# Graph attention edge pass: attention scores of four chunks in fourteen on VectorE instead of TensorE

## The reference, cut to what matters

```
x1  = layernorm(x)                      # per node, over 768
ft  = x1 (per head) @ W.T               # 12 heads, 64 -> 64
a1  = sum(ft * attn_l, -1)              # source score, one number a head
a2  = sum(ft * attn_r, -1)              # target score, one number a head
e   = leaky_relu(a1[src] + a2[dst], 0.2)
w   = exp(e - segment_max(e, dst)[dst])
msg = w / segment_sum(w, dst)[dst] * ft[src]
x   = x + relu(segment_sum(msg, dst) + x1 @ W_res.T)
x   = x + ffn(layernorm(x))
```

## Time and profile before

| | before |
|---|---|
| median of 3 runs | 2722.25 us (2721.98 to 2723.72) |
| the profiled execution | 2722.58 us, of which its span is 2720.8 us |
| busy, share of the span: PE, PEld, DVE, ACT, POOL | 97%, 88%, 88%, 87%, 78% |
| granted TensorE clock, mean | 0.989 of full |

### The profile page before, as it was taken

The page is one execution under the profiler, slowest core; times in us unless marked ns, Lnnn a source line. Parts: engine busy times, 40 slices in busy tenths (PEclk is TensorE's granted clock), DMA queues, the critical chain, the costliest instruction groups (busy, mean ns, idle before and its releaser), DMA issues. The chain is left out here.

```text
span 2720.8 us, 69258 instructions
## 1 busy us (share of the span) xinstructions
PE 2628.0 (97%) x21450; PEld 2389.0 (88%) x21450; DVE 2397.0 (88%) x4890; ACT 2378.5 (87%) x4748; POOL 2135.0 (78%) x2029
## 2 busy tenths in 40 slices
PE   5999999999999985999999999999999999999998
PEld 4888888888888864899999999999999999999997
DVE  4688888888888876999999999999999999999996
ACT  4988888888888863999999999999999999999993
POOL 7777777777777615888888888888888888888882
PEclk9999999999999997999999999999999999999999
DMA  8677777787777646899999999999999999989883
GB/s 314 215 259 254 254 252 253 252 252 253 254 253 255 217 149 245 313 350 341 333 332 330 324 321 324 324 317 315 317 321 314 314 319 315 311 312 312 315 311 119
DMA packets 254177, 777.86 MB, mean 286 GB/s; under 512 B 77185, under 2 KB 85165, under 8 KB 253837
## 3 DMA queue, kind: packets, MB, share of 16 engines
q1 hardware_dynamic: 184190, 563.88, 58.4%
q0 software_dynamic: 69312, 210.37, 25.0%
q10 hardware_dynamic: 432, 0.62, 0.1%
HBM read 638.86 MB, written 236.65 MB: 322 GB/s over the span
## 5 line engine op out<-in xcount | busy, mean ns | idle before, releaser
L1017 PE MATMUL ps<-wr_bd,arena 128*128 128x128 f32 x4704 | 592.7, 276 | 19.1 <-DVE arena L1390 19.0
L1017 PEld LDWEIGHTS ps<-wr_bd,arena 128*128 128x128 f32 x4704 | 563.0, 193 | 20.5 <-issue 20.4
L702 POOL DMA_INDIRECT arena<-agg_scratch,nrow x392 | 438.9, 1120 | 76.7 <-issue 67.5
L644 POOL TENSOR_SCALAR arena<-csr_neg,mv,r_n 128x768 f32<-128x768 f32 x392 | 388.2, 990 | 50.9 <-PE ps L859 37.9
L1385 DVE SCALAR_TENSOR_TENSOR ps<-ps,r_n,arena 128x768 f32<-128x768 f32 x392 | 398.9, 1018 | 16.6 <-DMA arena<-agg_scratch,nrow 15.5
L809 ACT ACTIVATE t_hi<-ps 128x768 fp32r<-128x768 f32 x392 | 314.3, 802 | 95.4 <-PE ps L859 95.2
L818 ACT ACTIVATE arena<-arena,s_st 128x768 f32<-128x768 f32 x392 | 363.6, 928 | 30.5 <-DVE arena L1390 30.5
L1390 DVE SCALAR_TENSOR_TENSOR arena<-ps,arena 128x768 f32<-128x768 f32 x392 | 375.3, 957 | 13.4
L692 POOL TENSOR_SCALAR arena<-arena,nm_n,r_n 128x768 f32<-128x768 f32 x392 | 382.6, 976 | 2.7 <-issue 1.9
L1397 DVE TENSOR_TENSOR t_lo<-ps,t_hi 128x768 fp32r<-128x768 f32 x392 | 373.7, 953 | 10.2 <-ACT t_hi L809 10.2
L777 ACT ACTIVATE arena<-arena,mv 128x768 f32<-128x768 f32 x392 | 367.4, 937 | 12.8
(11 more groups left out here) (213 smaller groups left out, 6218.9 us busy)
## 6 DMA issues: line engine op xcount, KB each, us to landing
arena<-in_x SPq DMA_DIRECT2D x196, 768.0 KB
arena<-in_x_cols SPq DMA_DIRECT2D x392, 384.0 KB, 5.0
out<-arena SPq DMA_DIRECT2D x195, 768.0 KB, 5.7
agg_scratch<-agg_ring SPq DMA_DIRECT2D x196, 384.0 KB, 3.8
dst_all<-in_dst_rows SPq DMA_DIRECT2D x28, 256.0 KB, 3.7
arena<-agg_scratch,nrow POOLq DMA_INDIRECT x392
arena<-in_x,e_slot POOLq DMA_INDIRECT x364, 4.6
dst_all<-in_dst_rows SPq DMA_DIRECT2D x28, 192.0 KB
```

The source lines that it names most:

```text
L644: pool.tensor_scalar(g_ring[:, g, :].rearrange("p (c f) -> p c f", f=P), csr_neg[:, None, :].to_broadcast([P, NC, P]), mv1[:, w, 2 * (v % ...
L702: pool.indirect_dma_start(g_ring[:, g, :], None, agg_d, bass.IndirectOffsetOnAxis(nrow[:, v, 3:4], 0), bounds_check=EP - 1, oob_is_err=Fal ...
L1017: last = nc.tensor.matmul(res_ps(b, tr)[:, i * P:(i + 1) * P], xt_ring[:, g, i * P:(i + 1) * P], wr_bd[:], start=True, stop=True)
```

## The change

Of every fourteen chunks, those at positions 2, 5, 9 and 12 (OFF_PE; "off chunks" from here) get their target scores without TensorE:

- ScalarE copies the target row from SBUF to `both_t`, scaled by -1/768, and sums it while it copies, which gives the negative mean.
- VectorE, as the last or one of the last operations of that step, computes (row + negative mean) * `v2_row`, where `v2_row` holds the 12 vectors of 64 side by side, the same in all partitions ("the product"); in the next step it sums the 64 numbers of each head ("the reduction").
- TensorE leaves out the six transposes of the target row, and one step later the six score matmuls and the matmul L933; the copies of their results go too, on ScalarE L745 and one of three pieces of L735 (and half of another), on VectorE L1184.
- For all chunks `ve_d` now comes behind the aggregated row, not ahead of the copy of the scores.
- `v2_row` is made once, at the pass's start: a product and a copy of 768 columns on VectorE, two matmuls on TensorE.

By i mod 7 the transposes go at steps 0 and 4, the score matmuls and L933 at steps 1 and 5, and the copy of the scores at steps 2 and 6. The product is added to VectorE's steps 0 and 4, the reduction to its steps 1 and 5.

```diff
+OFF_PE = (2, 5, 9, 12)
...
# ScalarE, at the copies out of PSUM
-                        at_least(act, s_sc, ct - 1)
...
+                        at_least(act, s_sc, on_pe(b, i - L_TR - 1))
+                        if (i - L_TR - 2) % BODY in OFF_PE:
+                            at_least(act, s_a2c, ct - 1)
+                        if (i - L_TR) % BODY in OFF_PE:
+                            vd = (i - L_TR) % BODY
+                            act.wait_ge(s_tr, NBLK * ct + 1)
+                            nc.scalar.activation(both_t[:, v, 0:BLK], ps[:, 0, :], ACT.Copy).then_inc(s_etr, 1)
+                            act.wait_ge(s_tr, NBLK * ct + NBLK)
+                            nc.scalar.activation(both_t[:, v, BLK:D], ps[:, 1, 0:D - BLK], ACT.Copy).then_inc(s_etr, NBLK - 1)
+                            act.wait_ge(d_gd[vd % G], 16 * (2 * b + (i - L_TR) // G + 1))
+                            nc.scalar.activation(both_t[:, v, D:2 * D], xd_ring[:, vd, :], ACT.Copy, scale=-1.0 / D,
+                                                 accum_out=a2_all[:, vd // G, vd % G, HEADS:HM]).then_inc(s_mean, 1)
+                        else:
...
# TensorE
-                        for k in range(NBLK):
+                        for k in range(2 if v in OFF_PE else NBLK):
...
-                            for m in range(4 * k, 4 * k + 4):
+                            for m in range(4 * k, min(4 * k + 4, NC if v in OFF_PE else 2 * NC)):
...
-                    if exists(cf, EC):
+                    if exists(cf, EC) and (i - L_FT) % BODY not in OFF_PE:      # the score matmuls, and L933
...
-                    if exists(c - L_SQD, EC):
+                    if exists(c - L_SQD, EC) and (i - L_SQD) % BODY not in OFF_PE:
                         pe.wait_ge(s_a2c, c - L_SQD + 1)
...
# VectorE: ve_d goes from here ...
-                    gd = 2 * b + (i - L_VD) // G
-                    if (i - L_VD) % G == 0 and exists(gd, NG):
-                        w = (i - L_VD) // G % 2
-                        dve.wait_ge(s_sqd, G * (gd + 1))
-                        V.tensor_scalar(ve_d[:, w, :], q_d[:, w, :], 1.0 / D, EPS, ALU.mult, ALU.add).then_inc(s_ved, 1)
...
-                        dve.wait_ge(s_sct, c2 + 1)
-                        V.tensor_copy(a2_all[:, w, j, :], a2_ps).then_inc(s_a2c, 1)
+                        if v not in OFF_PE:
+                            dve.wait_ge(s_sct, on_pe(b, i - L_SQD) + 1)
+                            V.tensor_copy(a2_all[:, w, j, :], a2_ps).then_inc(s_a2c, 1)
...
# ... to behind the aggregated row, unchanged
...
# VectorE, behind the group work of steps 5 (its first copies) and 0, ahead of that of step 4
+                    cr = c - L_FT
+                    if exists(cr, EC) and (i - L_FT) % BODY in OFF_PE:
...
+                        dve.wait_ge(s_prod, off_pe(b, i - L_FT) + 1)
+                        V.tensor_reduce(a2_all[:, w, j, 0:HEADS],
+                                        both_t[:, v % 2, D:2 * D].rearrange("p (h d) -> p h d", d=DH), axis=AX.X, op=ALU.add)\
+                            .then_inc(s_a2c, 1)
+
+                    cp = c - L_TR
+                    if exists(cp, EC) and (i - L_TR) % BODY in OFF_PE:
...
+                        dve.wait_ge(s_mean, off_pe(b, i - L_TR) + 1)
+                        V.scalar_tensor_tensor(both_t[:, v % 2, D:2 * D], xd_ring[:, v, :], a2_all[:, w, j, HEADS:HM], v2_row,
+                                               ALU.add, ALU.mult).then_inc(s_prod, 1)
```

More of the change, by code:

```diff
@@ L59 @@
 HM = HEADS + 1
+OFF_PE = (2, 5, 9, 12)
+N_ON = BODY - len(OFF_PE)
 NBLK = 3
@@ L108, in settle, with on_pe, off_pe @@
     eng.nop(nofuse=True)
+def on_pe(b, i):
+    return N_ON * (b + i // BODY) + sum(v not in OFF_PE for v in range(i % BODY))
+def off_pe(b, i):
+    return len(OFF_PE) * (b + i // BODY) + sum(v in OFF_PE for v in range(i % BODY))
 def exists(t, n):
@@ L360, in gnn_ffn_kernel @@
         s_a2c = sem("s_a2c")
+        s_mean = sem("s_mean")
+        s_prod = sem("s_prod")
         s_mask = sem("s_mask")
@@ L731, in _ @@
                         at_least(act, s_ft, ct - 1)
-                        at_least(act, s_sc, ct - 1)
-                        for k in range(NBLK):
-                            act.wait_ge(s_tr, NBLK * ct + k + 1)
-                            nc.scalar.activation(both_t[:, v, k * BLK:(k + 1) * BLK], ps[:, k, :], ACT.Copy).then_inc(s_etr, 1)
+                        at_least(act, s_sc, on_pe(b, i - L_TR - 1))
[11 more added lines that the diff above has]
+                        else:
+                            for k in range(NBLK):
+                                act.wait_ge(s_tr, NBLK * ct + k + 1)
+                                nc.scalar.activation(both_t[:, v, k * BLK:(k + 1) * BLK], ps[:, k, :], ACT.Copy).then_inc(s_etr, 1)
                     cf = c - L_FT
@@ L867, in _ @@
                         v = (i - L_TR) % BODY
-                        for k in range(NBLK):
+                        for k in range(2 if v in OFF_PE else NBLK):
                             if k == 0:
                                 pe.wait_ge(s_norm, ct + 1)
-                            if k == 1:
+                            if k == 1 and v not in OFF_PE:
                                 pe.wait_ge(d_gd[v % G], 16 * (2 * b + (i - L_TR) // G + 1))
                             at_least(pe, s_etr, NBLK * (ct - 1) + k + 1)
-                            for m in range(4 * k, 4 * k + 4):
+                            for m in range(4 * k, min(4 * k + 4, NC if v in OFF_PE else 2 * NC)):
                                 src = xs_ring if m < NC else xd_ring
@@ L877, in _ @@
                                                            src[:, v, m % NC * P:(m % NC + 1) * P], ident[:])
-                            last.then_inc(s_tr, 1)
+                            last.then_inc(s_tr, NBLK - 1 if k == 1 and v in OFF_PE else 1)
                     cf = c - L_FT
@@ L930, in _ @@
                                          ft_ring[:, v, 4:NC, 0:P], start=True, stop=True).then_inc(s_sum, 1)
-                    if exists(cf, EC):
-                        pe.wait_ge(s_esc, cf + 1)
+                    if isinstance(b, int) and c == L_TR:
+                        pe.wait_ge(s_v, 6)
+                        nc.tensor.matmul(sum_ps[:, 0:512], ones[:], v2_row[:, 0:512], start=True, stop=True)
+                        nc.tensor.matmul(sum_ps[:, 512:D], ones[:], v2_row[:, 512:D], start=True, stop=True).then_inc(s_pre, 1)
+                    if exists(cf, EC) and (i - L_FT) % BODY not in OFF_PE:
+                        pe.wait_ge(s_esc, on_pe(b, i - L_FT) + 1)
+                        if isinstance(cf, int) and cf == 0:
+                            pe.wait_ge(s_v, 7)
                         nc.tensor.matmul(a2_ps, sc_row, sel3, start=True, stop=True).then_inc(s_sct, 1)
@@ L1196, in _ @@
                             .then_inc(s_eo, 1)
+                    gd = 2 * b + (i - L_VD) // G
+                    if (i - L_VD) % G == 0 and exists(gd, NG):
+                        w = (i - L_VD) // G % 2
+                        dve.wait_ge(s_sqd, G * (gd + 1))
+                        V.tensor_scalar(ve_d[:, w, :], q_d[:, w, :], 1.0 / D, EPS, ALU.mult, ALU.add).then_inc(s_ved, 1)
                     cm = c - L_MSG
```

26 lines of the change are left out of this document (20 added, 6 removed).

## The result

| | before | changed |
|---|---|---|
| median of 5 runs each, side by side | 2722.87 us (2721.98 to 2727.90) | 2709.44 us (2707.67 to 2711.00) |
| ratio, 95% interval | | 0.9946 [0.9935, 0.9956] |
| profiled execution, span | 2720.8 us | 2707.6 us |
| granted TensorE clock, mean | 0.989 | 0.989 |

The change makes the kernel 13.4 us faster, and the interval leaves out 1. I had forecast 2729, 6.6 us slower. The time lies inside the range of 2708 to 2745, close to its lower end, but on the other side of no change.

What follows compares the result with a forecast made beforehand. TensorE bounded the edge pass at 34.56 us a group; a ring of waits through VectorE and TensorE would make it 34.87. 24.6 groups x 0.31 = 7.6, drain -2.5, start +1.5: +6.6, 2729 us, range 2708 to 2745.

Steps and rivals of the forecast that it cites:

- The ring: VectorE from step 4 to step 1, then TensorE or ScalarE back to step 4: 34.87 us a group; chance 0.60.
- The rival in which it doesn't close: Edge pass: TensorE not held at step 1, ScalarE not late, VectorE alone bounds at 33.5; 2695 us, chance 0.22.
- half gain: Partial case of VectorE alone bounding the edge pass: half of the -26 us, giving 2708 us.
- item 1: VectorE from the scores' copy at step 4 to the one at step 1: 22.24 us, new work included.
- The rest: From the scores' copy at step 1 to that at step 4: 7.55 + 4.89 + 0.19, 12.63 us.
- 34.56: Edge pass before the change: period in us of a group of seven steps, taken as bounded by TensorE.
- the start: Pass's start: two 768-column operations on VectorE, two matmuls on TensorE; taken as +1.5 us, between 0 and 3.3.
- the drain: Steps 196 to 204, without VectorE statistics: TensorE bounds again, gain between nothing and 4.1 us, taken as -2.5.
- 19.47: VectorE's old work from step 4's scores' copy to step 1's, less listed waits: mean of 19.90 and 19.04 us.
- Two ways of one length: From step 1's scores' copy to step 3: 7.55 us through TensorE's sum, 7.52 through ScalarE's late normalization.
- the 0.60: Chance given to a group period of 34.6 to 35.6 us, a sixth of it within 0.2% of no change.
- The rival of a product at half rate: VectorE's product takes twice the time per column: 36.6 us a group, 49 us more, 2770 us; chance 0.05.

Runs made afterwards that it cites:

- f1: Changed kernel with VectorE's short copy of e_row at step 5 replaced by a reduction over 768 columns, same values; 2727.98 us, ratio 1.0014.
- f2: Changed kernel with VectorE's short copy of dst_slot at step 3 replaced by a reduction over 644 columns; 2711.55 us, ratio 0.9953.
- a7: Changed kernel with other off chunks: products at the ends of steps 1 and 2, reductions in 2 and 3; 2686.61 us, ratio 0.9864.
- a8: Changed kernel with other off chunks: products in steps 2 and 3, reductions in 3 and 4; 2686.21 us, ratio 0.9865.
- e3: Changed kernel with product and reduction cut to 12 columns, so off chunks' target scores aren't computed; 2664.34 us, ratio 0.9783.
- e4: Kernel before with four added VectorE reductions of 768 columns a group, at steps 0, 1, 4, 5, TensorE's work unchanged; 2747.80 us, ratio 1.0084.
- a6: Changed kernel with nm_s computed at the end of step 0 ahead of the product, not at step 1's start; 2704.93 us, ratio 0.9931.
- e1: Changed kernel with one more VectorE reduction of 768 columns a group, at the end of step 5; 2789.42 us, ratio 1.0238.
- e2: Changed kernel with one more VectorE reduction of 768 columns a group, at the end of step 3; 2776.51 us, ratio 1.0193.
- t1: Changed kernel with one more VectorE reduction a group at step 3, of only 12 columns; 2774.07 us, ratio 1.0182.

## Why the prediction was wrong

**The mechanism was right.** The ring closes as numbered: TensorE waits at the sums of steps 6 and 1, most at step 1; VectorE waits at step 4 only, 1.47 where 1.4 was forecast; products of 1.01; no clock lost. f1, f2, a7 and a8 show that the ring sets the time. The rival in which it doesn't close gives a time near the measured one with its half gain, 2708, but for another reason: every wait that it denies is there.

**The step that failed is item 1, VectorE's way.** It was forecast at 22.24 and took 21.51 (mean of 21.14 and 21.88), 0.73 less. The rest was forecast at 12.63 and took 12.74. So the ring is 34.25 instead of 34.87, and 0.62 x 24.6 is 15.3 us of the 19.6 by which the time fell short. The margin to 34.56 was 0.31, less than this mistake, so the forecast came out with the wrong sign. The rest lies in the start (3.0), the drain (0.6) and what comes after it (0.9), which makes 19.8 in the spans.

The prices of the new instructions weren't it: 0.93 and 0.86 against 0.93 and 0.87 (the tenth that I took off the reduction's lower bound for the writes saved shows in no run). It was the 19.47 that the way took before "without its waits", of which the changed kernel needs only 18.8: 21.51 less the new instructions and `ve_d`, with the copy of the scores put back. Before, at the mask of step 4, the copies of step 5 and `nm_s` of step 1 in the group of 484.31:

```profile
487.45 0.27 DVE L1262 TENSOR_SCALAR arena<-dst_all,dst_slot 128x128 f32<-128x128 int32 x1
488.75 0.17 DVE L1287 TENSOR_TENSOR nmd<-a_all,r_d 128x7 f32<-128x7 f32 x1 [1.03 <-POOL r_d L590]
...
492.66 0.26 DVE L1262 TENSOR_SCALAR arena<-dst_all,dst_slot 128x128 f32<-128x128 int32 x1
493.00 0.29 DVE L1268 COPY e_row<-ps 84x128 f32<-84x128 f32 x1
493.21 0.28 DVE L1269 COPY same_r<-ps 84x128 f32<-84x128 f32 x1
493.52 0.35 DVE L1300 TENSOR_SCALAR pen_r<-same_r 84x128 f32<-84x128 f32 x1
493.91 0.42 DVE L1302 TENSOR_TENSOR_SCAN f_row<-pen_r,e_row 84x128 f32<-84x128 f32 x1
...
504.12 0.15 DVE L1162 SCALAR_TENSOR_TENSOR nm_s<-mvs,r_s 128x7 f32<-128x7 f32 x1
504.29 0.18 DVE L1170 COPY e_slot<-e_all 128x28 int32 x1
```

Between the same starts before and after (new instructions taken out at their own length):

| from, to | before | after | gained | subtracted in the forecast |
|---|---|---|---|---|
| mask to `nmd` | 1.30 | 0.18 | 1.12 | 1.03 |
| mask to `e_row` | 0.34 | 0.22 | 0.12 | 0 |
| `same_r` to `pen_r` | 0.31 | 0.20 | 0.11 | 0 |
| `pen_r` to first scan | 0.39 | 0.24 | 0.15 | 0 |
| `nm_s` to `e_slot` | 0.17 | 0.07 | 0.10 | 0 |
| `ve_d` | - | 0.07 | | added as 0.15 |

The gains not subtracted make 0.57, the price of `ve_d` 0.08, in sum 0.65 of the 0.67 missing in this half (21.81 forecast for it, 21.14 measured). In the other half (22.67 forecast, 21.88 measured) 0.79 are missing. The gains are of three kinds:
- *A wait is longer than its row says.* The idle time is counted from the end of the record before it, but back to back the next instruction starts about 0.1 before that end. Subtracting 1.03 leaves 0.09 too much. It happens again at the 0.40 and the 0.43 of the earlier trace rows, 0.08 and 0.09 in the other half.
- *Short waits have no row.* The 0.12 in front of `e_row` is listed nowhere, and it went like the long ones. That VectorE is now later than its suppliers is the likely reason, not a tested one.
- *The new work fills gaps.* `pen_r`, which reads `same_r`, came 0.31 after it; with the reduction in between, that begins after 0.20. The gap behind `nm_s` shrank by 0.10 with the product ahead of it. Other runs bear both out: in a7, with nothing between `same_r` and `pen_r`, and in e3, with an instruction of 12 columns there, it is 0.31 or 0.32 as before, though VectorE waits for no other engine there. Behind `nm_s` it is 0.15 to 0.20 in e3, a7 and a8, and 0.07 to 0.08 wherever an instruction of 768 columns stands ahead (e4, f1 and the changed kernel).

The 0.15 behind `pen_r` belongs to none of them. It points at something that I had overlooked: the group of 484.31 is an odd one. The waits of before in 300 to 700 us have `nmd` waiting only once, and the plain group from 415.19, which is like the others, waits in other places:

```profile
DVE nmd L1287 <- POOL r_d L590: 1.0, 1, 1.0
```

```profile
420.07 0.17 DVE L1184 COPY a_all<-ps 128x13 f32<-128x13 f32 x1 [0.39 <-PE ps L933]
...
423.89 0.29 DVE L1268 COPY e_row<-ps 84x128 f32<-84x128 f32 x1 [0.36 <-ACT arena L745]
```

In the other ten groups of those 400 us the first scan comes 0.25 or 0.26 after `pen_r` before, and 0.24 or 0.25 now. The way from 415.19 is 20.15, less its two listed waits 19.40, which is 0.36 more than the 19.04 taken for this half. So with an ordinary group the forecast would have been further off, 22.17 against 21.14 for this half; the waits and gaps not listed are then spread over some ten places, as 0.15 between the mask and `nmd`, 0.17 between the mask and `alpha`'s first operation at step 0, and 0.09 in the messages of step 4.

e4 checks this on the kernel before: with three reductions of 0.86 on the way and one wait of 0.22, its plain half took 21.48, which leaves 18.68 for the old work, against the 19.04 that I had used for that half: 0.36 less, with TensorE's work as it was. In the changed kernel it is 18.44.

**Start and drain.** The drain was forecast at -2.5 and gave -3.1. The start was forecast at +1.5, between 0 and +3.3, and gave -1.5: outside my bounds, and with VectorE's two and TensorE's two new operations in it. No experiment was aimed at it, and what gives these 3 us stays open. `nmd` surfaced nowhere in the changed kernel, as forecast; in e3 and a7, without the product ahead of it, it did.

**Two ways of one length.** I had put TensorE's at 7.55 and ScalarE's at 7.52 from step 1's copy to step 3. Step 3 begins 371.38 - 363.71 = 7.67 after it, and a6, which relieves ScalarE alone, brings the rest down by 0.22. So ScalarE's was the later.

**The chances.** The weak point was theirs too. The two halves of the way differed by 0.86 after the subtraction (19.04 and 19.90), and the result hung on 0.31. So the old work was the widest unknown of the sum, but the range of the ring (34.54 to 35.56) held the bounds of the new instructions alone. With it, a good part of the 0.60 belonged below 34.56. The rival of a product at half rate, which is also the rule of the Trainium skill's "Vector Engine (DVE) Microarchitecture Reference", "Points that are easy to get wrong", is out: 1.01 us for 768 columns with two SBUF sources (345.98 above), as much as the aggregated row takes with one in PSUM (342.68); the trace doesn't agree with the rule.

## What to carry to other kernels

Work moved to another engine costs what it adds to the longest way between two waits, not what it adds to the engine: the same four instructions a group gave 13 us in one place and 38 in another. Find the place where the engine waits in each period and put the new work in front of it, and check by making a short instruction there long. A time "without its waits" is best added up from the starts of instructions that follow each other without a wait, and not got by subtracting the listed waits; and over several periods, since a single one can be odd.

## What the runs showed of the hardware

- The first VectorE instruction of a loop body came 0.2 to 0.4 us late at each turn in the kernels whose body has as many instructions as the changed kernel's or fewer, and 4.0 to 5.6 us late in e1, e2 and t1, whose body has one reduction more in each of its two groups (by the order of the programs, 230 lines against 232). One such instruction a group, of 12 columns, cost 65 us in all (t1). What runs out there the trace doesn't name, and where the limit lies no run tells.
- The granted clock fell with these stalls: in 300 to 700 us it was 0.96 in e1, e2 and t1, and about 0.975 over the whole of each. In the changed kernel, where TensorE has 23 us of gaps in those 400, but none over 1.4 us, it stayed at 1.00, the level of 2.4 GHz. So the 65 us hold some time of the clock as well; how much was not taken apart.
- A product of two float32 rows in SBUF (`scalar_tensor_tensor`, 128x768) took 1.01 us by its record and 0.93 in a chain, the same as with one row in PSUM; a reduction of 768 columns to 12 took 0.94 and 0.86.
